# Row maxima of score tiles taken two tiles at a time, over two neighbouring banks

## What is computed

```python
# layer 0; layer 1 differs in the groups, the biases and the skip
xn = _group_norm(x, gn_scale, gn_bias)
qkv = jnp.einsum('bhwc,cd->bhwd', xn, w_qkv)
...
scores = jnp.einsum('bcq,bck->bqk', q, k) * hd ** (-0.5)
scores = jax.nn.softmax(scores, axis=-1)
o = jnp.einsum('bqk,bck->bqc', scores, v)
...
out = jnp.einsum('bhwc,cd->bhwd', o, w_out) + b_out
return out + skip
```

## Time and profile before

| | |
|---|---|
| median of 3 runs | 2081.41 us |
| profiled execution | 2081.65 us |
| its span | 2079.9 us |
| PE busy | 2035.4 us (98%) |
| DVE busy | 1669.9 us (80%) |
| ACT busy | 1489.1 us (72%) |
| POOL busy | 414.5 us (20%) |
| instructions | 40626 |

### The profile page before, as it was taken

How to read it: one execution, slowest core, us unless ns; L and a number is a source line. 1 busy time by engine, 2 the same in 40 slices (tenths; PEclk the granted TensorE clock), 3 DMA queues, 4 the chain that set the end, 5 groups by cost and what they waited for, 6 DMA issues and landing times.

```text
span 2079.9 us, 40626 instructions
## 1 busy us (share of the span) xinstructions
PE 2035.4 (98%) x15688; PEld 1148.1 (55%) x15688; DVE 1669.9 (80%) x3104; ACT 1489.1 (72%) x2722; POOL 414.5 (20%) x544
## 2 busy tenths in 40 slices
PE   5899999999999999999999999999999999999999
PEld 3344444443744477444874448644585446847988
DVE  5999999998799878898789886898878977873433
ACT  1577788887588855988569885697747986497555
POOL 4102111220122311122120221202112031031231
PEclk8899999999999999999999999999999999999999
DMA  5503242341222214041230502304031031000000
GB/s 145 107 2 78 53 87 55 60 89 15 61 54 62 43 32 81 12 86 19 57 67 2 103 2 64 60 2 103 2 85 29 3 78 26 12 2 2 11 1 21
DMA packets 48591, 97.40 MB, mean 47 GB/s; under 512 B 7824, under 2 KB 10640, under 8 KB 48272
## 3 DMA queue, kind: packets, MB, share of 16 engines
q1 hardware_dynamic: 48400, 94.81, 21.4%
HBM read 55.98 MB, written 37.75 MB: 45 GB/s over the span
## 4 chain that ended last, share of the span: by engine, by line
PE 85%; DVE 11%; issue 1%; ACT 1%; POOL 1%; DMA 0%; SPq 0%; POOLq 0%; DVEq 0%; ACTq 0%
PE outs L1473 21%; PE banks L1435 15%; PE banks L1448 12%; PE outs L1513 11%; DVE part_max L1227 9%; PE banks L1491 9%; PE banks L1354 7%; PE banks L1360 5%; PE banks L1363 4%; ACT probs L1117 1%; DVE stats L1166 0%; PE banks L1421 0%; DVE o_turn L1239 0%; DMA avg<-averages 0%; DVE oT L1254 0%
## 5 line engine op out<-in xcount | busy, mean ns | idle before, releaser
L1227 DVE TENSOR_REDUCE part_max<-banks 128x1 f32<-128x512 f32 x2048 | 1270.2, 679 | 164.7 <-PE banks L1435 159.0
L1117 ACT ACTIVATE probs<-banks 128x512 f32<-128x512 f32 x2048 | 1059.3, 610 | 184.5 <-PE banks L1448 156.9
L1473 PE MATMUL outs<-probs,v_heads 128*32 128x512 f32 (+1 forms) x5088 | 561.6, 522 | 2.1 <-ACT probs L1117 1.0
L1435 PE MATMUL banks<-k_stack,q_stack 62*128 62x512 f32 x2048 | 550.7, 441 | 6.7 <-issue 2.5
L1448 PE MATMUL banks<-q_stack,k_stack 64*128 64x512 f32 x2048 | 518.4, 443 | 4.2 <-DMA q_stack<-shift_parts 1.9
L1435 PEld LDWEIGHTS banks<-k_stack,q_stack 62*128 62x128 f32 x2048 | 257.3, 186 | 288.3 <-DVE part_max L1227 115.5
L1448 PEld LDWEIGHTS banks<-q_stack,k_stack 64*128 64x128 f32 x2048 | 244.1, 185 | 218.1 <-DVE part_max L1227 82.5
L1124 ACT ACTIVATE probs<-banks,neg_max 128x1024 f32<-128x1024 f32 x128 | 142.8, 1116 | 214.4 <-DVE neg_max L1259 182.4
L1513 PEld LDWEIGHTS outs<-v_full,probs 128*128 128x128 f32 x2048 | 256.9, 191 | 44.4 <-issue 33.7
L1513 PE MATMUL outs<-v_full,probs 128*128 128x128 f32 x2048 | 275.3, 278 | 0.0
L1259 DVE TENSOR_REDUCE neg_max<-banks 128x1 f32<-128x1024 f32 x128 | 156.3, 1222 | 128.3 <-PE banks L1491 127.3
(11 more groups left out here) (107 smaller groups left out, 1121.3 us busy)
## 6 DMA issues: line engine op xcount, KB each, us to landing
k_scratch<-parts SPq DMA_DIRECT2D x64, 256.0 KB
q_scratch<-parts SPq DMA_DIRECT2D x64, 256.0 KB
k_stack<-k_scratch SPq DMA_DIRECT2D x64, 256.0 KB, 6.5
q_stack<-q_scratch SPq DMA_DIRECT2D x64, 256.0 KB, 8.7
k_stack<-k_scratch SPq DMA_DIRECT2D x64, 128.0 KB, 8.4
q_stack<-q_scratch SPq DMA_DIRECT2D x64, 128.0 KB, 9.8
q_stack<-shift_parts SPq DMA_DIRECT2D x256, 4.0 KB
tmp<-x SPq DMA_DIRECT2D x7, 512.0 KB, 3.9
```

The lines of the kernel that those rows point to most:

```text
L1117: nc.scalar.activation(probs[:, plan.prob[u], 2 * n + half, :], banks[:, plan.banks["pair", t][k], :], ACT.Exp, scale=HEAD_SCALE).then_inc ...
L1227: nc.vector.tensor_reduce(part_max[:, r % 2, column:column + 1], bank_of(("tile", r, n)), AX_X, ALU.max, negate=True).then_inc(tile_max, 1)
L1435: nc.tensor.matmul(bank_of(("tile", r, n)), qs[rows, i, a, heads, P * t:P * (t + 1)], ks[rows, i, keys, heads, :], start=True, stop=True). ...
L1473: last = nc.tensor.matmul(outs[2 * HD * n:2 * HD * (n + 1), columns], v_heads[:, i, key, at:at + 2 * HD], probs[:, plan.prob[u], n, column ...
```

## The change

Tiles now come in couples. `Plan` keeps only the even tile numbers, so a tile step stands for the tiles n and n + 1, the two heads of one block. A couple takes two neighbouring banks (`DOUBLES`) and waits for both before its first matmul. The two matmuls go into the two halves of PE's rows one after the other, and only the second signals `tile_full`. DVE reduces both banks with one instruction: input 128 x 2 x 512, output two columns of `part_max`. Its one `tile_max` signal frees both banks. A pair now always begins with half 0, since a couple always ends with half 1. The two tables have new letters.

```diff
+        if item[0] == "tile":
+            return [self.take(DOUBLES[part], item)]
...
+        self.order = [c[:2] + (c[2] - 1,) if c[0] == "tile" else c for c in self.order if c[0] != "tile" or c[2] % 2]
         self.order = self.arranged(self.order)
...
-                rows = item[2] % 2
+                rows = 1
...
-        "TCCCPTPTTTPTUTPTU TTPTUTPTU TTPTUTPTU TTPTCUTPTU TTPTCUTPTU HTPTUTPTU TTPTPUTTU TPTPCUTTU CTPTTPTV TPTTPV "
+        "CCCPTPTPTUPTU TPUTPU TPTUPTU TPCUTPU TPTCUPTU HPTUPTU TPPUTU TPPCUTU CTPTPV TPTPV PTPTV PTPUTU PTPUTU HPPTV "
...
                     dve.wait_ge(tile_full, t + 1)
-                    column = TILES // 2 * (n % 2) + n // 2
-                    nc.vector.tensor_reduce(part_max[:, r % 2, column:column + 1], bank_of(("tile", r, n)),
+                    first = plan.banks["tile", r, n][0]
+                    nc.vector.tensor_reduce(part_max[:, r % 2, n // 2:TILES:TILES // 2], banks[:, first:first + 2, :],
                                             AX_X, ALU.max, negate=True).then_inc(tile_max, 1)
-                    if n == TILES - 1:
+                    if n == TILES - 2:
...
-                def score_tile(r, n):
+                def score_tiles(r, n):
...
-                    nc.tensor.matmul(bank_of(("tile", r, n)), qs[rows, i, a, heads, P * t:P * (t + 1)],
-                                     ks[rows, i, keys, heads, :], start=True, stop=True).then_inc(tile_full, 1)
+                    for half in range(2):
+                        rows = slice(ROWS * half, ROWS * (half + 1) - SHIFT)
+                        last = nc.tensor.matmul(banks[:, plan.banks["tile", r, n][half], :],
+                                                qs[rows, i, a, heads, P * t:P * (t + 1)],
+                                                ks[rows, i, keys, heads, :], start=True, stop=True)
+                    last.then_inc(tile_full, 1)
```

More of the change, by code:

```diff
@@ new lines @@
+        "TPPUU TPTV PTCCPPTTV TPCCV PTHPTPTV PPTTV PTUTPPCU CCTPTV PTTCCPTV TPPV CCCTTPUCCCTPTCU TPTCV HPTTCPTUPTU "
+        "PPCCV TPPCCV CCPTPV CPTTPUTPPPTTU UU TPTV TCCPTV THPTPTPTV PPTTV TPPV CPPTUU PTPTTPV PTTPV UPPTTU V "
+        "HPTPTTPV PPTTV PTPTV CPPTV PTPTCV PPTTV PTPTUU PTPCUHPTU TPTV PTTPV TTPUPU CPPTV TPUCPTTCCCCCU PTTUU "
+        "PTPTCPPTCCCPTTV HCPTV TTCCCCPPTV CCPV PTPTCUCPTU PCPTPCV PTCPV PTTV CTPV PTTCPTV PTTCHCTPTV PTV TPTCPTV "
+        "CPTPCUTPTCCPTU TPV PTPV PPTV TPHPTPTV TPTV PTTCTCUPPU PTUU CPTPUTPTPPU TTPV CCPPTTUU PTCV HPTTV CCUPTPU "
@@ new lines @@
+        "TPUU PTPTUU PTPV PTPV CPTTUCPTU PPTTUCTPU CCCCPTV HPTPCUTPTCU CTPV TPPCCCCCTPTV TPV PTPCCCV CPPTTV CPTPTV "
+        "PPTUPPTU TCUPTTCU HPTPV PTPV CCPTTV V PTPPCTPCV PTPTPTV PTTPV CPPCTPUU TPTV UHPTPCU PTTCCV TPPV PTCCPTTCV "
+        "PTCTPPV CPTV TPCPTPV PTPV PTPV V HPTTSV CSTR TTCGR SGCGTTGR SSGSGGR GYSGR CCGGGTTTGGGGCCR YTTGGSGSGCR "
+        "CGGGTTTGCYCCSR SGGGGCR GGGTTGCR YSHCGGGGTTCCGGR TGSGCCR YCSGTGR GGTCTGR SGGGYSGCTGR GGTTPGGGGYR "
+        "PGGGCTTGGGPTGGPYTTCV PTPUTPPU TTTV HCCPPTV CPTPV TPTCUTPCPTPU TV PPTUU CCPPTV TPPV PPTTV PTPTV HPPTV PTPTV "
@@ new lines @@
+        "TPCPTCV PPTUPU CPPTV CTUPTU CPTTV PTPCTPPV PPTV PTPPV TPTUHPTU V PCPTV PPTTV PTPTV PTPV CTPPCV PPTV PPTV "
+        "TPTV PCCTPTV HPTPCCPTTUCU CCTPPV CPTTCTCCCPTUPTU TPV TPPCV CCCPTCCPV TPPV CPTPCV PTPTUHPPTTU V CPPTTTCPPTV "
+        "TCCPPV TPPV V TPPUU CCPTPTV PTPTUU PTPV PTPCUU PCTPV HPPTV CCPTPV TPTCCTPTV CCPTPV TPCCTPPV TPTV TPCPTV "
+        "PTPV TPPV PTTV PHSV CTSR SCR TGGGTTTCGGR SGSGGYSGR CGTTGR GSGCGTTGGCYR SGGGCGTTTCGCGGR SGCR CYSGCTTGGSGCR "
+        "TGGGGCYTTHR GGCSGSGCR GCGGTTGCCYR SCTTCGGGGGGR R GGYTTSGSGGTGR CTPGGGGYCTR TPGGGGGGPTGGYPTTCV PTPV "
@@ new lines @@
+        "SGTTGGGCCR R YCGGTTGSGSSGCR GGGR YTTCGGGGTTPGGGGR YPTGGCGGTTGGPTGGPYTTCV PTPV TPCCTPPV TTHCCPTPV PTPV PTTCV "
+        "PTPV TPTUU PCPPTTUU PPTV PPTV PPTV TPTCV HPTPTPPV TTCPV PCTPUU PCTPTCV PPTV PTPV PPTTV PTPTUU PTPUU "
+        "CHPPTCTV PTPTV CPPTV PTPCV PPTCV PPTUU PTPTPPV TPTV PTUU PTPV PCTTCPV HTPTCPTV PTCPV TPCCCPTCCTTPV "
+        "CCTPPCCCTPCCV PTPV TPTV CTCPV CPTPUU PPTV PTPV CHPPTTV CPTCTPTCCPPV PTTTV PV TPPV CCPTPV PTPV CPPTV PCTTPV "
+        "PPTV HPTPV PTTCV CTTPCCPTPV CPPTCV TPTCPTCV PTPV PTTUPCTPPU V PTPV TPPV STTV HCR SCSGGCGR TGTTTGGSR SGGYR "
@@ new lines @@
+        "PTPTUU PTPV TPPCV PTPV TPPV SV CTSR CSCR GGGTTTGGGR SGTGYSR SGGGTTGGR TGSGSGYR R GGGGGTTTGGHR "
+        "GYSTSGGTTGGGSGR R GGYSGGTGR TTGGSGCR CGGR YSSGGGGGCTTTGGGYR SCTGGR GCGTTPGGGGYCTR HPTGGGGGGTPGGPPYTCV "
+        "PTTCPTV PTV PPTCV TPCCPTPV PTPCV TPTV TPV PCPTPUU TTPV HPPTPV TPPV TPTUU PTCPTUPU CPTPV TPPV CPTPV CTPTV "
+        "CCPTPTPPV PPTCV HPPPV CPPCV V PPUU CPPPV CPPCV PPUCPPU UCCPPU V PPPUU V SV CSR CSCR SGGSGR R GGGGGYSGGGSGGR "
+        "R GGGYSGGSGR GGR GGGYSGGSGGGR GGGYCSGR GCCGSGR GGGCR CGYR SGGGGCSGGCGGR YCGGCGR CCGGSGSGGCYSGR GGGSGGR R "
@@ L204 @@
+        "GGYR SGGGCGGGCSGGCR YSGGCSGR GGCCGGCGR YCGGCCCR SGSGGGGGYR R GGSGGSGGGGR YCSGGGGR CSGGGGR YCCSGGGGR CSGGGGR "
+        "YCCCCSGGGGR CCSGGGGR YSGGGGR SGGGGR YSGGGGR SGGGGR YSGGGGR SGGGGR YSGGGGR GGGGR YGGGGGGGGY "
     )
@@ L1424, in shift @@
                     last.then_inc(bank_full, 1)
-                def score_tile(r, n):
+                def score_tiles(r, n):
                     first, a, i = heads_of(r)
-                    heads, t, keys, half = first + n // (2 * KT), n // 4 % QT, n // 2 % 2, n % 2
-                    rows = slice(ROWS * half, ROWS * (half + 1) - SHIFT)
+                    heads, t, keys = first + n // (2 * KT), n // 4 % QT, n // 2 % 2
                     if n == 0:
@@ L1544, in _ @@
                     elif kind == "tile":
-                        score_tile(*item[1:])
+                        score_tiles(*item[1:])
                     elif kind == "shift":
```

76 lines of the change are left out of this document (19 added, 57 removed).

## The result

The changed kernel takes 2143.26 us (median of 4 runs, 2139.99 to 2145.75) beside 2081.76 us of the kernel before on the same chip: 1.0295 times as long, with a 95% interval of 1.0282 to 1.0308. The prediction said 2062 us and a range of 2034 to 2100. The sign was wrong. PE's mean granted clock, in shares of full speed, is 0.990 in both profiles, so the clock has no part in it.

The account below looks back on a forecast made before the run. PE was taken as near the bound throughout, with DVE's maxima the pace before 520 us. Maxima -15, odd runs -23.4, more runs +4 and banks +15 gave -19 us: 2081.65 to 2062 us, range 2034 to 2100.

Parts of the forecast that it names:

- Odd runs: PE's runs of tile and pair matmuls all become even, saving 33.6 us of PE; 23.4 us after 520 us counted.
- at 1.13 to 1.14 us: Sign of being right: PE's runs of eight tile and pair matmuls take this long, with no odd runs left.
- Banks held longer: A couple's first bank comes free 0.54 us later, so PE's weight loads wait: +15 us, between 0 and 45.
- Signals and waits: Fewer PE signals, but couples wait for two banks before their first matmul: taken as 0, up to +11 us.
- Maxima: DVE's 1024 two-bank maxima take 1222 ns, 1143 ns apart, saving 57 ns a couple: -15 us before 520 us.
- DVE below 1620 us: Sign of being right: DVE's busy time over the program falls below 1620 us, from 1669.9.
- The bank ring: Rival: couples wait 0.54 us for banks still being reduced, giving 2107 us, or 2092 with DVE's saving; chance 0.22.
- The gain moves to ACT: Rival: PE's 23.4 us after 520 us become waits for exponentials, no change, 2079 to 2086 us; chance 0.12.
- DVE's idle time before 520 us: Sign of being wrong: DVE's idle time before maxima between 42 and 520 us grows from 19 us.
- the waits for exponentials: Sign of being wrong, pointing to ACT: PE's weight loads wait far above 164 us for exponentials.
- The sum of waits for maxima: PE's weight loads: not above 198 us was a sign of being right, far above it of being wrong.
- More runs: PE has 734 runs of tiles and pairs instead of 714, at 0.20 us each: +4 us; values split about as often.

Follow-up runs that it names:

- x3: The change with maxima over the first 256 of 512 columns and most exponentials over 256 of 512; 2059.98 us, 0.9898 of the kernel before.
- x4: The kernel before with maxima over the first 256 of 512 columns and most exponentials over 256 of 512; 2036.16 us, 0.9781 of the kernel before.
- e1: The change's order of steps, but each tile with its own bank, wait, signal and maximum; 2134.98 us, 1.0255 of the kernel before.
- x1: The change with each maximum over the first 256 of a tile's 512 columns, exponentials whole; 2114.64 us, 1.0158 of the kernel before.
- e6: The change with joint wait, joint PE signal and neighbouring banks, but two maxima, each freeing its bank; 2152.08 us, 1.0351 of the kernel before.
- e2: The change with couples put off so that a run has at most three couples (six matmuls); 2248.22 us, 1.0818 of the kernel before.
- e5: e1 with any tile that would be a run's eighth matmul put off behind the next other step; 2183.9 us, 1.0496 of the kernel before.
- e8: The change with half a values step put into the middle of 59 of the 89 runs of eight; 2157.46 us, 1.0369 of the kernel before.
- e12: The kernel before with tiles that would make a run longer than 6 put off, 583 moved; 2218.47 us, 1.0653 of the kernel before.
- e4: The kernel before with six banks instead of seven; 2325.76 us, 1.1178 of the kernel before.
- x2: The kernel before with each maximum over the first 256 of a tile's 512 columns; 2067.25 us, 0.993 of the kernel before.

## Why the prediction was wrong

**Odd runs: the step that failed.** The runs were counted rightly: -33.6 and +4 in the prediction, -29.6 in the table, which is the same formula over the runs of the trace. With short reads the runs of up to 7 lie only 9.4 us (x3) and 2.3 us (x4) above the price in all, so 0.20 + 0.235 for each two is what such a run costs when banks are free. Wrong was the line drawn on to runs of eight "at 1.13 to 1.14 us". The changed order has 114 runs of eight and more, 40 were there before; a run of eight took 1.84 us on average (89 of them). The 40 of before lay 37.9 us above their price, 0.95 each; 74 more of them would have been some +70 us, and at the least 0.53 each (the 1.67 of the shortest less 1.14), +39. Either value added to the forecast's -19 would have given a slower kernel. Measured, the time in runs of tiles and pairs rose by 20.3 + 60.5 - 29.6 = 51 us instead of falling. The rows for it were in the trace of before, and the run lengths in the order; the prediction looked only at whether runs were odd.

**Banks held longer.** Taken at +15 (0 to 45) for first banks that come free 0.54 us later. That mechanism is the small one: e1, without any joint release, has lost 55 of the 62 us already. What e1, x1 and x3 show is another form of shortage: with both tiles at one place four banks and more are asked for at once. The short runs' 20 us over their price are of that kind too: the difference shrinks to 7 when maxima and exponentials are short (x3 against x4). The Trainium skill, "TensorEngine Tiling (Array Packing)", section on restrictions and gotchas, says that tiling by rows raises the pressure on PSUM; these runs agree with it.

**Signals and waits.** Taken at 0 (up to +11). With the neighbouring banks that a joint wait asks for it is +17 (e1 to e6), above the +11. The 351 added double waits and the narrower choice of banks weren't taken apart.

**Maxima.** Duration 1219 and pace 1.145 us, as worked out (1222, 1.143), and DVE below 1620 us was missed by 2. But the -15 us in the first 520 us weren't to be had: DVE waited there for PE. By itself, beside tiles that are side by side already, the joint maximum is worth 9 us over the whole program (e6 to the change), with its longer hold paid. The rule of the Trainium skill, "VectorE: DVE Perf Modes", section on the TRN2 errata, by which a couple would save an estimated 125 ns (120 cycles at 0.96 GHz), is not borne out by the pace: two maxima of 0.60 us against 1.145 leave 55 ns.

**The rivals.** The bank ring had the sign and the resource, at 2092 to 2107 us. It was priced by counting waits of the old order, so it couldn't contain the runs that the new order makes. "The gain moves to ACT" named the row that did grow (exponentials, 164 to 228 us), but as a cap on the gain; it is a loss, since what PE waits for in 84 of the 89 runs of eight is their own exponentials.

**The signs named beforehand.** DVE's idle time before 520 us (57.2 from 19.0) and the waits for exponentials pointed the right way, and so did runs of eight at 1.84 us and PE's longer time in tiles and pairs. The sum of waits for maxima fell from 198 to 133 us, and by the text that would have been a sign of success: PE waited elsewhere first. One count was misread without consequence: the 238 and 248 of "More runs" are halves of values steps, so 119 and 124 steps are split.

**What stays open.** Whether an order made anew with couples and no run longer than six or seven would keep the 29.6 us. e2, e5 and e8 cut runs by a simple rule, and e12 shows that such a rule alone can cost 137 us. Nor is it known what makes the values 6 us dearer in the change, and 10 in x3. No version here that computes everything is faster than the kernel before.

## What to carry to other kernels

A price per run, read from runs that fit into the buffers, ends where a run asks for more buffers than there are: count the places first, and look for the few cases in the old trace that already go beyond. Work that is put side by side to save on one engine asks for its buffers side by side too, so each step that is moved is to be priced by what it asks for at that moment, not only by what it issues. And a stall that is cut out of one stretch in a ring that is short throughout comes back in the next, so an experiment that only removes the stall says little about the cause; shortening the readers, or taking a buffer away, does.

## What was not expected of the hardware

The part of a run that asks for one bank too many starts 0.55 to 0.76 us after what stands before it, not 0.235 (the timelines above): 1.13 us at seven matmuls with seven banks, 1.77 at eight, and 1.71 already at seven with six banks (e4). One maximum over two neighbouring banks with two results takes as long as one with a single result over 1024 columns (1219 and 1223 ns, the latter for line 1251 after), so the second result costs nothing that shows:

```profile
L1251 DVE TENSOR_REDUCE neg_max<-banks 128x1 f32<-128x1024 f32 x128 | 156.5, 1223 | 131.1 <-PE banks L1486 130.1
```

And halving the columns of every maximum takes only 14 us off the kernel before (2081.22 to 2067.25) though it frees DVE of 1270.2 - 749.1 = 521 us of work; x2's row:

```profile
L1227 DVE TENSOR_REDUCE part_max<-banks 128x1 f32<-128x256 f32 x2048 | 749.1, 416 | 502.6 <-PE banks L1435 497.1
```
